# A dilated convolution in 3 tiles of 8 outputs from 14 points, instead of 4 tiles of 6 from 12

## The reference

```
k    = relu(conv(ln(x), w1, 7x7 taps, dilation 2, padding 6) + b1)      # 256 -> 128 channels
k    = relu(batchnorm(conv(k, w2, 1x1) + b2))                           # 128 -> 49, one per tap
attn = softmax(k, axis=1)
out  = sum over the 49 taps p of shifted(ln(x), p) * attn[:, p]
x    = x + out
```

## Time and profile before

| | |
|---|---|
| profiled execution, span from first to last instruction | 999.0 us |
| runs | 999.81, 1001.24, 1005.07 us |
| PE busy | 927.6 us (93%) |
| DVE busy | 732.0 us (73%) |
| ACT busy | 543.3 us (54%) |
| line 1273, the convolution's matmuls | 2016, 323.4 us busy |
| bytes moved by DMA | 96.02 MB, mean 96 GB/s |

### The profile page before, as it was taken

How to read it: one execution, slowest core, us unless ns; L and a number is a source line. 1 busy time by engine, 2 the same in 40 slices (tenths; PEclk the granted TensorE clock), 3 DMA queues, 4 the chain that set the end, 5 groups by cost and what they waited for, 6 DMA issues and landing times. The chain is left out here.

```text
span 999.0 us, 18982 instructions
## 1 busy us (share of the span) xinstructions
PE 927.6 (93%) x7395; PEld 708.7 (71%) x7395; DVE 732.0 (73%) x1817; ACT 543.3 (54%) x985; POOL 147.5 (15%) x165
## 2 busy tenths in 40 slices
PE   2887999999999999979999947999999999999997
PEld 2776666777677667646999934777777777777776
DVE  4797466368647844977579857778978897888877
ACT  4795334435344512223456438576867777686751
POOL 1110000000000010100213221111211121122112
PEclk9998999999999999989999868999999999999999
DMA  9813111004101105454458446354255335424211
GB/s 219 215 48 95 49 48 48 25 5 129 53 25 53 39 24 157 144 161 89 115 151 231 126 127 143 95 126 95 62 152 106 64 80 159 97 53 92 64 33 48
DMA packets 135112, 96.02 MB, mean 96 GB/s; under 512 B 63611, under 2 KB 129548, under 8 KB 134924
## 3 DMA queue, kind: packets, MB, share of 16 engines
q1 hardware_dynamic: 135022, 94.81, 37.1%
HBM read 55.95 MB, written 29.40 MB: 85 GB/s over the span
## 5 line engine op out<-in xcount | busy, mean ns | idle before, releaser
L1273 PE MATMUL pM<-V,U 128*128 128x368 f16 (+3 forms) x2016 | 323.4, 316 | 0.0
L1273 PEld LDWEIGHTS pM<-V,U 128*128 128x128 f16 x2016 | 195.7, 98 | 103.2 <-issue 2.3
L1963 DVE SCALAR_TENSOR_TENSOR gl<-gf,sc,gh 128x384 f16<-128x384 f32 x192 | 147.9, 807 | 51.6 <-ACT gh L1776 51.5
L1785 ACT ACTIVATE gf<-pH,b1c,sc 128x384 f32<-128x384 f32 x192 | 127.8, 669 | 89.2 <-issue 73.4
L2094 PE MATMUL pH<-xT,w1h 128*128 128x384 f16 x768 | 158.2, 329 | 6.9 <-DMA xT<-xs 4.5
L2110 PE MATMUL pY<-w2h,gl 128*128 128x256 f16 x576 | 157.0, 273 | 0.0
L2110 PE MATMUL pY<-w2l,gh 128*128 128x256 f16 x576 | 157.0, 273 | 0.0
L2110 PE MATMUL pY<-w2h,gh 128*128 128x256 f16 x576 | 157.0, 273 | 0.0
L745 ACT CAST V<-pV 128x384 f16<-128x384 f32 x96 | 45.7, 478 | 156.3 <-PE pV L1244 156.3
L901 DVE TENSOR_TENSOR V<-pV,V 128x384 f16<-128x384 f32 x96 | 52.0, 552 | 88.6 <-ACT V L745 88.3
L1776 ACT ACTIVATE gh<-gf,sc 128x384 f16<-128x384 f32 x192 | 115.4, 616 | 0.0
(11 more groups left out here) (259 smaller groups left out, 1335.7 us busy)
## 6 DMA issues: line engine op xcount, KB each, us to landing
xa<-in_xt SPq DMA_DIRECT2D x16, 576.0 KB, 6.6
xs_scratch<-xs SPq DMA_DIRECT2D x16, 576.0 KB, 3.9
tk<-t_scratch SPq DMA_DIRECT2D x24, 384.0 KB, 3.9
out<-o SPq DMA_DIRECT2D x23, 384.0 KB, 2.9
xs<-in_ew SPq DMA_DIRECT2D x16, 512.0 KB, 4.2
U<-xs_scratch SPq DMA_DIRECT2D x16, 480.0 KB, 4.8
w1r<-in_ew SPq DMA_DIRECT2D x8, 512.0 KB, 4.3
w2r<-in_ew SPq DMA_DIRECT2D x8, 512.0 KB, 5.3
```

Source lines behind the costliest of these rows:

```text
L1273: return nc.tensor.matmul(out[:, :, first:end], U[:, k, hi_u, piece, :], V[:, b % 2, hi_v, k, c, :, first + TILES * d:end + TILES * d], st ...
L1785: nc.scalar.activation(gf[:, (JB * m + j) % GBUFS, :], pH[:, (JB * m + j) % HBUFS, 0:CN], ACT.Gelu, bias=b1c[:, j // FB, j % FB:j % FB + 1 ...
L1963: stt(gl[:, sl, j, :], gf[:, (JB * m + j) % GBUFS, :], scale_of(G_UP), gh[:, sl, j, :], ALU.mult, ALU.subtract).then_inc(g_step, 1)
```

## The change

`MO` goes from 6 to 8: three tiles a row, 14 points, six pairs. A product of a round then has 288 columns instead of 384, a data turn 168 instead of 192, a tap turn 224 instead of 192. Data turns are placed in the first 12 of 14 rounds (`V_SLOTS`). `EARLY_SLOTS` is moved by two rounds, from 7..11 to 9..13, with the same numbers; `UNITS_SLOT` stays. The tables `U` and `Gs` grow, so memory is laid out again: two of the spread matrices move from `V` to `U`, the homes that `X` is loaded back to are moved, and of the eight weight tiles six have a home of their own; the last two are loaded into those of the first pair, once `u_turned` says that its seven tap turns are done.

```
-MO = 6
+MO = 8
 TILES = SIDE // MO
-POINTS = [p for a in (1.0, 0.625, 1.5, 0.375, 3.0) for p in (a, -a)] + [0.0]
+POINTS = [p for a in (1.0, 0.53125, 1.65625, 0.28125, 3.15625, 1.15625) for p in (a, -a)] + [0.0]
 NP = len(POINTS) + 1
...
+W_HOMES = 6
...
-W_IN_V = 5
+W_IN_V = 4
...
-Y_STEPS = 2 + 8 * (PAIRS - 1) + 2
+Y_EACH = 2 + MO
+Y_STEPS = 2 + Y_EACH * (PAIRS - 1) + 2
...
-EARLY_SLOTS = {(7, 0): 4, (7, 1): 4, (8, 0): 4, (8, 1): 4, (9, 0): 3, (9, 1): 3, (10, 0): 3, (10, 1): 3, (11, 0): 3, (11, 1): 2}
+EARLY_SLOTS = {(9, 0): 4, (9, 1): 4, (10, 0): 4, (10, 1): 4, (11, 0): 3, (11, 1): 3, (12, 0): 3, (12, 1): 3, (13, 0): 3, (13, 1): 2}
...
+    V_SLOTS = V_TURNS * BI // 2
...
-            homes = ((Vf[0], (0, 0)), (Vf[0], (0, 1)), (Vf[0], (-1, 0)), (Uf, (1, 0)), (Uf, (-1, 1)), (Uf, (1, 1)))
+            homes = ((Vf[0], (0, 0)), (Vf[0], (0, 1)), (Uf, (-1, 0)), (Uf, (-1, 1)), (Uf, (1, 0)), (Uf, (1, 1)))
...
-            for g in range(2, OGS):
+            for g in range(2, W_HOMES):
                 load_w(sp, g)
             for i in range(BI):
                 store_xs(i)
                 load_x(i + XBUFS)
+                if i == 0:
+                    sp.wait_ge(u_turned, U_PAIR)
+                    for g in range(W_HOMES, OGS):
+                        load_w(sp, g)
...
             for b in range(B):
                 for k in range(NP):
                     m = V_TURNS * BI * (b + 1) + 2 * k
-                    if b < B - 1:
+                    turns = b < B - 1 and k < V_SLOTS
+                    if turns:
                         v_low(m)
...
                     for c in range(CC):
-                        if b < B - 1:
+                        if b < B - 1 and k < V_SLOTS:
                             turn_v(V_TURNS * BI * (b + 1) + 2 * k + c)
```

More of the change, by code:

```diff
@@ L60 @@
 OG = 16
-W_IN_V = 5
+W_HOMES = 6
+UC, VC = 2 * OG * NP, 2 * VCOLS
+W_IN_V = 4
 DATA_BITS, TAP_BITS = 11, 14
@@ L250, in mix_phase @@
         xa = xall[0:TT]
-        work = sb("work", [P, 12 * BW + 2 * MAP], F32)
+        work = sb("work", [P, (6 + MO) * BW + 2 * MAP], F32)
         E = sb("E", [TT, BI, NT * TAPS + EPAD - TAPS], F32)
@@ L257, in mix_phase @@
         Td = sb("Td", [TT, 2, VCOLS], F16)
-        Gt = sb("Gt", [OG * KS, NP * OG], F32)
         st = sb("st", [TT, 2, NT, 6], F32)
@@ L263, in mix_phase @@
         sized = sb("sized", [TT, IMGS, NT], F32)
-        sizes = sb("sizes", [TT, IMGS, NT], F32)
+        sizes_all = sb("sizes", [P, IMGS, NT], F32)
+        sizes = sizes_all[0:TT]
+        bsplit = sizes_all[:, :, :].rearrange("p n t -> p (n t)")[:, 0:TAPS]
         order = sb("order", [TT, TT], F32)
@@ L275, in mix_phase @@
         bias_ones = sb("bias_ones", [P, TT], BF16)
-        bsplit = sb("bsplit", [P, TAPS], F32)
         ones = sb("ones", [P, P], F32)
@@ L280, in mix_phase @@
         sg = sb("sg", [P, PAIRS_OG, 4], F32)
-        dg = sb("dg", [OG * KS, 2, OG * KS], F32)
         back_w = sb("back_w", [CMID, 1], F32)
[L284 to L288, removed]
+        ydata = work[:, 0:MO * BW]
+        sd = work[:, MO * BW:(MO + 4) * BW].rearrange("p (a s n) -> p a s n", a=2, s=2)
+        msb = work[:, (MO + 4) * BW:(MO + 6) * BW].rearrange("p (a n) -> p a n", a=2)
+        aTs = work[0:TAPS, (MO + 6) * BW:].bitcast(F16).rearrange("p (i a n) -> p i a n", i=2, a=2)
+        at = (MO + 6) * BW
         ln_rows = work[0:IMGS * NT, at:at + 2 * TT].rearrange("p (w x) -> p w x", w=2)
@@ L311, in mix_phase @@
         for g, (_, imgs, _) in enumerate(GROUPS):
-            homes = ((Vf[0], (0, 0)), (Vf[0], (0, 1)), (Vf[0], (-1, 0)), (Uf, (1, 0)), (Uf, (-1, 1)), (Uf, (1, 1)))
+            homes = ((Vf[0], (0, 0)), (Vf[0], (0, 1)), (Uf, (-1, 0)), (Uf, (-1, 1)), (Uf, (1, 0)), (Uf, (1, 1)))
             for k, (flat, part) in enumerate(homes):
-                home = (0, 0, 0, 2, 2, 2)[k] if g == 0 else 3
+                home = (0, 0, 2, 2, 2, 2)[k] if g == 0 else 3
                 A[g][part], ends[home] = spread_part(flat if g == 0 else Vf[1], ends.get(home, 0), part[0], imgs)
@@ L319, in mix_phase @@
               Uf[:, ends[2]:ends[2] + BI * MAP].rearrange("p (i x) -> p i x", i=BI)]
-        at = 5 * UP + G_COLS
-        assert ends[2] + BI * MAP <= at and G_COLS <= UP
+        at = ends[2] + BI * MAP
+        A_FREE = -(-at // UP)
+        assert G_COLS <= UP and ends[0] <= UP * NP and ends[3] + (TSB // 2) * 2 * NB * C <= 2 * NP * CC * BI * ROWT
         XT = 2 * NB * C
-        acc = Uf[0:TB, at + 2 * XT:at + 2 * XT + 4 * (B - ADDED) * C].bitcast(F32).rearrange("p (b a c) -> p b a c", a=2, c=C)
-        X_HOMES = [at, at + XT, (NP - 3) * UP, (NP - 2) * UP]
+        ACC = 4 * (B - ADDED) * C
+        acc = Uf[0:TB, at + 2 * XT:at + 2 * XT + ACC].bitcast(F32).rearrange("p (b a c) -> p b a c", a=2, c=C)
+        X_HOMES = [at, at + XT, at + 2 * XT + ACC, at + 3 * XT + ACC]
         X = [Uf[0:TB, h:h + XT].rearrange("p (t a c) -> p a t c", a=2, t=NB) for h in X_HOMES]
         X_rows = [Uf[0:TB, h:h + XT].rearrange("p (t x) -> p t x", t=NB) for h in X_HOMES]
-        G_FREE, A_FREE, X_FREE = 1, 6, [-(-(h + XT) // UP) for h in X_HOMES]
-        assert at + 4 * XT <= (NP - 3) * UP
+        G_FREE, X_FREE = 1, [-(-(h + XT) // UP) for h in X_HOMES]
+        assert at + 4 * XT + ACC <= (NP - 2) * UP - UP + XT, (at, XT, ACC, UP)
         small = [Uf[:, (NP - 3 + s) * UP + XT:(NP - 2 + s) * UP].bitcast(F32) for s in range(2)]
@@ L463, in halves @@
             return (whole, tile[:, 0:NB - 1, :]), (dram[at + (NB - 1) * TB:at + PIX, :], tile[0:TL, NB - 1, :])
[L465 to L468, removed]
+        w_homes = ([V[:, 1].rearrange("p b k c i n -> p (b k c i n)").bitcast(F32)[
+                       0:OG * KS, g * KS * C:(g + 1) * KS * C] for g in range(W_IN_V)]
+                   + [work[0:OG * KS, g * KS * C:(g + 1) * KS * C] for g in range(W_HOMES - W_IN_V)])
+        wst = [w_homes[g % W_HOMES] for g in range(OGS)]
+        at = (W_HOMES - W_IN_V) * KS * C
+        Gs = work[0:OG * KS, at:at + UC].rearrange("p (a n) -> p a n", a=2)
+        Gt = work[0:OG * KS, at + UC:at + UC + NP * OG]
+        dg = work[0:OG * KS, at + UC + NP * OG:at + UC + NP * OG + 2 * OG * KS].rearrange("p (a n) -> p a n", a=2)
         spots = U[:, :, :, :, CMID - 2 * OG:CMID].bitcast(F32).rearrange("p k a z n -> p (k a z) n")
@@ L477, in u_in @@
             banks = pA if u % 2 else pM[:, 0:2]
-            return banks[:, :, 0:BW].rearrange("p z (k n) -> p z k n", n=2 * OG)
+            return banks[:, :, 0:UC].rearrange("p z (k n) -> p z k n", n=2 * OG)
         def v_place(m):
@@ L488, in v_in @@
         def v_in(m):
-            return pV[:, m % 2, 0:BW].rearrange("p (k x) -> p k x", k=NP)
+            return pV[:, m % 2, 0:VC].rearrange("p (k x) -> p k x", k=NP)
         def y_pair(b, p):
-            return b * Y_STEPS + (2 if p == 0 else 8 * p - 4)
+            return b * Y_STEPS + (2 if p == 0 else Y_EACH * (p - 1) + 4)
         def shifted(b, i):
@@ L575, in _ @@
             load_x(0)
-            sp.dma_start(Gt[:, :], tap_d).then_inc(tap_loaded, 16)
+            sp.dma_start(Gt, tap_d).then_inc(tap_loaded, 16)
             sp.dma_start(Td[:, :, :], data_d).then_inc(tab_loaded, 16)
@@ L755, in copy_m @@
                 elif b > 0:
-                    act.wait_ge(y_step, y_pair(b - 1, (4, 3)[p]))
+                    act.wait_ge(y_step, y_pair(b - 1, PAIRS - 2 + p))
                 nc.scalar.activation(msb[:, p % 2, :], pM[:, (NP * b + 2 * p) % 3, 0:BW], ACT.Copy,
@@ L933, in tap_scale @@
                     dve.wait_ge(u_turned, U_PAIR * (pair - 1))
-                s.did(nc.vector.tensor_scalar(Gs[:, pair % 2, :], Gt[:, :], t[0:OG * KS, 3:4], None, ALU.mult))
+                s.did(nc.vector.tensor_scalar(Gs[:, pair % 2, :], Gt, t[0:OG * KS, 3:4], None, ALU.mult))
                 s.did(nc.vector.tensor_copy(back_w[mine, :], t[mine, 2:3]))
@@ L943, in y_points @@
             def y_points(b, p, between=()):
-                s = Steps(dve, y_step, b, Y_STEPS, 0 if p == 0 else 8 * p - 6)
+                s = Steps(dve, y_step, b, Y_STEPS, 0 if p == 0 else Y_EACH * (p - 1) + 2)
                 dve.wait_ge(m_copied, PAIRS * b + p + 1)
```

## The result

The changed kernel takes 992.82 us, the median of 20 executions, against 1001.22 us before: a ratio of 0.9909, 95% interval 0.9892 to 0.9925. It is faster by 8 to 10 us, where 15 were forecast; 986 was 0.7% too low. Its executions lie further apart than those of before (986.6 to 998.2, without one that was disturbed). The first profile is of an execution near the upper end (998.17 us, span 996.4), so the same kernel was profiled again (`after_again`, span 987.4). Both are used: what they share comes from the change, and where they differ one has to ask.

The account below looks back on a forecast made before the run. PE's matmul stream bounds batches 0 to 2, DVE's list the last batch, a chain setup. Terms +4 - 9.3 - 3.2 - 3.2 - 3.2 = -14.9 against span 999.0 give 984.1, with the median 2.2 above: 986; range 971 to 997.

Parts of the forecast that it names:

- Products: PE's matmuls on 288 columns: a half round falls from 3.18 to 2.40 us, still at column rate.
- third rival: PE's product spacing doesn't fall with width, so the kernel gets slower: 1056 us; chance 0.05.
- DVE's tight places: Batches 1 and 2: PE waits for DVE in rounds 5, 7 and 9, 6.2 us a batch.
- The clock after a wait: Batches 1 and 2: PE falls to half speed after some waits over 2 us, +1 us a batch.
- Batches 1 and 2: PE's gain of 10.4 us less waits and clock loss: -3.2 us each, bounds -10.4 and -0.4.
- Setup: Wider tap turns and DVE work lengthen setup by 4 us, bounds 2 and 7.
- cover for the weight tiles: Setup: late loading of the last two weight tiles, 11 us, hidden by some 35 us, costing nothing.
- The last batch: DVE's list decides, first spread piece at about 65.6 us: -3.2 us, bounds -9.1 and +1.5.
- The rest: The remaining 520.60 us, holding nothing the diff edits: left unchanged.
- First rival: DVE's lists stay hidden and PE bounds every batch: -36 us, 965; chance 0.10.
- Second rival: Waits in batches 1 and 2 cost half speed, last batch gains nothing, setup pays 7: 1000 us; chance 0.15.

Follow-up runs that it names:

- short_alow: Changed kernel leaving out most of the attention maps' low parts (DVE's a_low) in batches 1 and 2: 984.11 us, ratio 0.9818.
- maps_late: Changed kernel with the attention maps of batches 1 and 2 turned in later rounds, no work left out: 980.93 us, ratio 0.9778.
- v_early: Changed kernel with DVE's second v_low placed right behind the pair's outputs in even rounds from 2 on: 995.6 us, ratio 0.9931.
- maps_early7: Changed kernel with maps of batches 1 and 2 turned late and the last batch's spread table from round 7 on: 974.78 us, ratio 0.9719.

## Why the prediction was right, and where not

- *Products.* Right. 2.42 us a half round against 2.40, 0.115 us each, so at full speed 2016 x 151.3 ns before and 2352 x 115.2 ns after make 34 us less, with 336 products more. The third rival is out. An estimate from the two figures of the Trainium skill ("TensorE: Matmul & The Clock Gate", Back-to-back issue gap) is 99 ns at this width and 111 before. Both traces are above it, and their fall, 36 ns, is three times its 12.
- *DVE's tight places.* Right in place and size: 2.1, 0.8, 2.1 and 1.2 us were worked out for rounds 5, 5, 7 and 9; the second profile has 2.12, 0.81, 2.24 and 1.08. The prediction blamed DVE's lists, and `short_alow` and `maps_late` show that. It described them by the last `v_low` that PE waits for, which is only where the surplus surfaces: `v_early` moved that and won nothing.
- *The clock after a wait.* I took one half-speed stretch in each of batches 1 and 2. The first profile has it (the clock is 0.98 there), the second has none after waits of the same length, and the batches differ by 0.6 us. So the term of +1 a batch was 0.6 in one execution and nothing in the other.
- *Batches 1 and 2* are 0.5 to 1.1 us longer than the sum. In the second profile, where the +1 for the clock did not come, 1.5 us are to be explained: half rounds of 2.42 instead of 2.40 are 0.6, a wait of the logits' matmul 0.3, and 0.6 is not traced. PE's waits there, all of batch 2:

```profile
PE pV L1259 <- DVE V L915: 5.4, 3, 2.2
PE pA L1345 <- DVE mx L1004: 0.8, 1, 0.8
PE pL L1325 <- DVE mx L1004: 0.3, 1, 0.3
```

- *Setup.* +3.3 and +3.7 against +4. Kernels with the same setup took 95.8 to 98.7 us here, and its idle times were not traced further. The cover for the weight tiles held.
- *The last batch* is the step that failed: -3.2 forecast, -0.3 and +2.3 measured. The mechanism was right (the maxima and the pair that the moved table puts ahead of the first piece), and both ways to undo it give 5 us; its size was too small. The first piece came after 66.8 and 68.6 us, not 65.6: waits for the maxima's loads were 2.8 and 4.25 us, where I had left those of before (2.3), and 0.7 and 1.0 us more is DVE's work. From PE's restart to the stage's end it took 37.5 and 38.3 us, not 35.8. Half speed behind the long wait is not what was missed: it stood in the 43.2 us of before too (5.21 us for 21 products, now 3.95 and 4.70). But PE waited 1.70 us once for a piece that DVE had not done, 1.0 more than before at that place, and in the first profile the 21 products behind this wait ran slow as well (3.98 us instead of 2.58); the rest is not traced. The term's bound of +1.5 lies between the two profiles, so in the first the term was outside its own bounds. PE's two rows of the first profile:

```profile
449.08 0.49 PE L1376 MATMUL pV<-xa,U 113*128 113x60 f16 x8 [1.70 <-DVE V L1100]
449.41 3.98 PE L1288 MATMUL pM<-V,U 128*128 128x288 f16 x21
```

- *The rest* was costed at nothing. That holds for the second profile; in the first the clock alone made it +3.9. The median of the runs lies between.
- *First rival* (DVE's lists are hidden, 965): wrong as the kernel stands, and `maps_early7` shows how near it comes once DVE is relieved: 975.
- *Second rival* (DVE takes nearly all, 1000): the measured 992.82 lies about midway between it and the forecast, so the number alone does not decide; the stretches do. Batches 1 and 2 gained 2.1 to 2.7 us and not 0.4, and setup paid 3.3 to 3.7 and not 7. On the last batch the rival was right: it gained 0.3 us in one profile and lost 2.3 in the other.

## What to carry to other kernels

When the bounding engine is made faster, look for the stretch in which the next engine was just hidden, compare the two engines' busy time in that stretch and not over the stage, and expect the gain to stop where they cross. Here the waits went when work of the second engine was moved to rounds where it had room, and did not when the order was changed within the full stretch; the move, with the spread table back in round 7, made some 27 us out of 9. A table that says when background work is done has to be laid out anew when the rounds under it change.

## What the hardware did that was not expected

The same program had its attend stage at granted clocks of 0.87 and 0.91 in two executions, 5.2 us apart, though PE's work in it was the same. In the first profile the clock was at half speed (1.2 GHz) from 484.5 to 491.3 us; it fell during the last of 20 matmuls of a single column. Three matmuls of 256 columns took 0.85 us there and 0.49 elsewhere. PE's timeline there:

```profile
482.62 2.66 PE L1411 MATMUL pA<-U,xs 120*128 120x1 f32 x20
...
486.45 0.85 PE L1392 MATMUL pM<-U,V 120*120 120x256 f16 x3
...
492.12 0.49 PE L1392 MATMUL pM<-U 120*72 120x256 f16 x3
```

In the second profile the same sums for the same image were not followed by a fall; behind those of the next image the clock fell 1.1 us after their end. Likewise a wait of PE of 2.22 us was followed by products at half speed in the first profile (21 in 4.25 us) and one of 2.25 us at the same place in the second was not (2.58 us):

```profile
234.41 0.61 PE L1259 MATMUL pV<-Td,xs 96*128 96x168 f16 x6 [2.22 <-DVE V L915]
234.86 4.25 PE L1288 MATMUL pM<-V,U 128*128 128x288 f16 x21
```

```profile
233.47 0.61 PE L1259 MATMUL pV<-Td,xs 96*128 96x168 f16 x6 [2.25 <-DVE V L915]
233.91 2.58 PE L1288 MATMUL pM<-V,U 128*128 128x288 f16 x21
```

What decides it, the runs do not show. It means that a difference of a few us between two profiles is first looked for in the clock.
